# A two-layer graph transformer on one core: the gate's bias added by VectorE, its tangent taken in SBUF, and the attention terms turned ahead of the output projection

## The chip, the cores and the metric

The kernel runs on one core of a Trainium2 chip. The metric is the time of one execution on the device in microseconds. The profile names the engines PE (TensorE; PEld is its weight load), DVE (VectorE), ACT (ScalarE), POOL (GpSimd) and SP (SyncE, which only issues transfers here).

## What is computed

`x` is 64 graphs of 128 nodes with 384 features, `adj` a 128 x 128 mask for each. Two layers follow one another, each with a residual and a layer norm. The first is masked attention with 6 heads of 64. The second is a graph attention with 12 heads of 32 and a gate:

```
h = einsum('bnd,ade->bane', x1, W); th = tanh(h)
attn = th·w_src + swap(th·w_dst);  attn = where(attn >= 0, attn, 0.2 * attn); masked, softmax
feat = elu(attn @ h + b)
gate = sigmoid(x1 @ H_w.T + H_b)
y = layernorm(x1 + gate * feat + (1 - gate) * x1)
```

All is f32. Products that need the full precision are made as three products of a high and a low part (hi·hi, lo·hi, hi·lo).

## The kernel before

One graph is one tile of 128 nodes, and the 64 tiles are written out one after the other in the program of every engine: groups of four (`g`, `j` = 0 to 3), 18 rounds in all. In a round, TensorE makes the q, k and v projections of the next group (`qkv`; `fill_a`, `fill_b`), the first layer's attention of a tile (`att`, tile `ta`), the second layer's projections and logits of a tile two behind (`gat`, `tl` = `ta` - 2) and the end of the one behind that (`tail`). The rounds at the end have no `qkv`, then no `att`. The tile j = 3 makes four v projections where the others make one q or k projection each for `ps_a` and `ps_b`. Every engine works through its list in order, and semaphores that are waited for in that list bind the engines together. The order is written by hand.

The second layer of a tile, as far as the change touches it:

- TensorE turns the tile (`turn_x1`, L409), multiplies it into `ps_d` bank 1 (h, L253) and, in three chunks between other work, into `ps_d` bank 2 (the gate). Behind the last chunk a bfloat16 product adds the gate's bias, held as three bfloat16 rows (L429).
- ScalarE takes tanh of h (`th`, L633); GpSimd multiplies it with the two weight rows (`thw`, L999); VectorE sums it (L844) and splits the sums into three bfloat16 terms (L868 to L878, `sd3`).
- TensorE turns the terms (`turn_sd`, L435). ScalarE makes `rows_L` of them (L670, three), VectorE makes `cols_R` (L885, on partitions 64 to 127).
- TensorE makes the logits (L447): three products, one for each of the banks 0, 1 and 2 of `ps_d`. These banks hold the turned weights of the tile before (`turn_p1`, L459) until they have been copied to `p1T` (bank 0 by VectorE, L760; banks 1 and 2 by ScalarE, L593).
- ScalarE takes the tangent of half the gate from `ps_d` bank 2 (L661). VectorE uses `gate` two tiles later (L824).

The wait in the logits reads:

```
for q in range(3):
    pe.wait_ge(S["rows_ready"], 3 * t + q + 1)
    if due(t):
        pe.wait_ge(S[f"p1T_{q}"], t)
```

In the lists around it, `L362` turns the first layer's weights, after GpSimd has normalised them (L991); VectorE copies them (`p0T`, L830); `L742` makes the low parts of the turned tile and of the context; L747 and L752 evict q and k from `ps_b`; L891 to L895 begin the last norm of a tile, which GpSimd ends, and GpSimd's mask addition on the logits (L964) stands behind that. Twice a group GpSimd also waits for the terms (`sd3_ready`) before it adds a bias to the next input (L945), and once before it makes the low part of the next group's input (L916, two).

Of the kernel before, what the change touches and what calls it, by code (L numbers as in the profile page):

```python
# [29 lines left out]
ALU = mybir.AluOpType  # L30
# [18 lines left out]
def build_program(nc, xT_in, x, adj, Wq, bq, Wk, bk, Wv, bv, Wf, bf, W1, b1, w_src, w_dst, HwT, Hb,  # L49
                  ident_in, pick_in, out):  # L50
    with ExitStack() as ctx:
# [23 lines left out]
        ones_b = sb("ones_b", [P, P], BF16)  # L75
# [12 lines left out]
        hb_rows = sb("hb_rows", [P, D], BF16)  # L88
# [43 lines left out]
        def staging(buffer):  # L132
# [4 lines left out]
        hb_row = r1[0:1, :]  # L137
        hb_rest = y[0:1, :, :]
        hb_split = gate[0:1, :, :].rearrange("p a d -> p (a d)").bitcast(BF16)[:, 0:3 * D].rearrange("p (a d) -> p a d", a=3)
# [4 lines left out]
        names = """padding_ready ident_in_ready const_in weight_in_0 weight_in_1 weight_in_2 weight_in_3 weight_in_4 weight_in_5 late_hi bvf_made bf_ready adj_in x_in_ready weight_hi weight_lo mask_ready consts_ready pick_ready hb_moved  # L144
            bias_in bias_ready hb_small x_hi x_lo x_lo_first xb_in xb_ready q_made k_made qk_a_ready qk_b_ready v_made v_even v_odd
            scores_ready neg_ready exp0_ready inv0_ready p0_ready p0_turned p0T_even p0T_odd
            ctx_made ctx_hi ctx_lo out_made r0_ready mv0_ready ln0_small x1_ready
            x1_turned x1_hi x1_lo h_made h_ready th_ready gate_made gate_ready thw_ready
# [47 lines left out]
        def _(sp):  # L196
            sp.dma_start(x_cols[:], xT_in[0]).then_inc(S["x_in_ready"], 16)
            for n, name in enumerate(W_ORDER):
                if n == 4:
# [6 lines left out]
                    sp.dma_start(hb_row, Hb.rearrange("(o d) -> o d", o=1)).then_inc(S["const_in"], 16)  # L206
# [41 lines left out]
        def _(pe):  # L248
            def split_product(out_ap, lhs, rhs, chunks=range(C), closed=True):

                for c in chunks:
                    for k, (a, b) in enumerate(HI_LO):
                        last = pe.matmul(out_ap, lhs(a, c), rhs(b, c), start=(c == 0 and k == 0),  # L253
                                         stop=(closed and c == C - 1 and k == 2))
                return last
# [156 lines left out]
            def project_h(t, n, j):  # L412
# [3 lines left out]
                if isinstance(t, int) and t == 0:  # L416
                    pe.wait_ge(S["weight_lo"], 6)
                    pe.wait_ge(S["hb_moved"], 16)
# [4 lines left out]
            def project_gate(chunks):  # L423

                split_product(ps_d[:, 2, 0:D], lambda a, c: x1T[a][:, c, :],
                              lambda b, c: w_parts["hw"][b][:, c, :], chunks, closed=False)
# [23 lines left out]
            def turn_p1(t, next_is_here, groups):  # L450

                for q in groups:
                    if next_is_here and q == 1:
                        pe.wait_ge(S["h_ready"], t + 2)
                    if next_is_here and q == 2:
                        pe.wait_ge(S["gate_ready"], t + 2)
# [23 lines left out]
            def iteration(g, par, n):  # L480
                qkv, att = parts(n)
                for j in range(G):
# [50 lines left out]
        def _(act):  # L533
# [25 lines left out]
            def iteration(g, par, n):  # L559
# [36 lines left out]
                for j in range(G):  # L596
# [68 lines left out]
                    if gat:  # L665
# [25 lines left out]
        def _(dve):  # L691
# [19 lines left out]
            def small_constants():  # L711
# [4 lines left out]
                dve.wait_ge(S["padding_ready"], 2)  # L716
# [4 lines left out]

                dve.tensor_copy(hb_split[:, 0, :], hb_row).then_inc(S["hb_small"], 1)
                dve.wait_ge(S["hb_small"], 1)
                dve.tensor_tensor(hb_rest[:, 0, :], hb_row, hb_split[:, 0, :], ALU.subtract).then_inc(S["hb_small"], 1)
                dve.wait_ge(S["hb_small"], 2)
# [331 lines left out]
```

## Time and profile before

| | |
|---|---|
| median of 3 runs | 1132.04 us (1130.24 to 1132.44) |
| the profiled execution | 1132.1 us, span 1130.2 us |
| busy | PE 1073.2 us (95%), ACT 919.4 (81%), DVE 897.2 (79%), POOL 765.2 (68%) |
| mean granted clock of TensorE | 0.986 of full speed |

The time of an execution is a little longer than the span between its first and last instruction. Busy time is that in which an engine has an instruction under way. Matmuls are pipelined and the end of one is modelled, so TensorE can read as busy through a short wait; the starts of its products and weight loads tell more.

### The profile page before, as it was taken

What the parts mean: (1) busy time and instruction counts of PE and PEld (TensorE: products, weight loads), DVE (VectorE), ACT (ScalarE), POOL (GpSimd) and SP (SyncE); (2) the same over time, 40 slices, a digit from 0 to 9 for tenths busy, and PEclk for the clock granted to TensorE, in tenths of its full rate; (3) what the DMA queues carried; (4) which work ended last, traced back from release to release, by engine and by line L of the source; (5) the groups of instructions that cost most, each with busy time, mean ns of one, the idle gap of its engine ahead of it and who ended that gap; (6) DMA issues with size and microseconds to landing.
All of it is one profiled execution on the core that took longest, in us unless ns stands there. A gap on an engine that the chain in (4) does not pass through costs nothing.

```text
span 1130.2 us, 25501 instructions
## 1 busy us (share of the span) xinstructions
PE 1073.2 (95%) x8236; PEld 883.3 (78%) x8236; DVE 897.2 (79%) x1828; ACT 919.4 (81%) x3383; POOL 765.2 (68%) x909
## 2 busy tenths in 40 slices
PE   6889999999999999999999999999999999997774
PEld 5678888888888888878888888888888888786652
DVE  5457878888887888888788888878888887888874
ACT  3348888888888888888888888888888888888874
POOL 1367776676777667677766767776676777667652
PEclk9999999999999999999999999999999999999986
DMA  9101010020101002010100201010020101000000
GB/s 270 56 2 57 15 68 18 8 71 16 64 15 61 26 8 71 16 64 15 62 26 8 71 15 64 15 60 27 8 72 16 64 15 43 16 8 16 16 15 21
DMA packets 25893, 44.66 MB, mean 40 GB/s; under 512 B 2462, under 2 KB 23714, under 8 KB 25762
## 3 DMA queue, kind: packets, MB, share of 16 engines
q1 hardware_dynamic: 23234, 41.91, 10.9%
q10 hardware_dynamic: 2496, 1.12, 0.5%
q8 instruction: 68, 1.11, 0.4%
q14 instruction: 63, 0.52, 0.2%
q0 software_dynamic: 32, 0.00, 0.0%
HBM read 30.43 MB, written 12.58 MB: 38 GB/s over the span
## 4 chain that ended last, share of the span: by engine, by line
PE 57%; POOL 23%; issue 9%; DVE 6%; ACT 3%; DMA 2%; POOLq 0%; ACTq 0%; DVEq 0%
PE ps_b L253 13%; PE ps_d L253 13%; POOL z L964 9%; PE ps_a L253 7%; PE ps_d L459 5%; POOL xT_lo L916 4%; PE ps_a L382 3%; PE ps_s L362 3%; PE ps_s L354 3%; PE ps_d L447 3%; POOL p L991 3%; PE ps_c L469 2%; POOL s L956 2%; POOL thw L999 2%; POOL y L958 2%
## 5 line engine op out<-in xcount | busy, mean ns | idle before, releaser
L583 ACT ACTIVATE z<-z,s 128x128 f32<-128x128 f32 x768 | 297.1, 391 | 1.5 <-DVE s L798 0.9
L964 POOL TENSOR_TENSOR z<-z,mask 128x512 f32<-128x512 f32 x192 | 218.2, 1164 | 0.5 <-ACT z L679 0.5
L583 ACT ACTIVATION_READ_ACCUMULATOR z<-z,s 128x1 f32 x768 | 146.6, 191 | 0.0
L610 ACT ACTIVATE p<-ps_s,s 128x128 f32<-128x128 f32 x384 | 134.7, 378 | 13.1 <-DVE s L776 13.0
L991 POOL TENSOR_TENSOR p<-p,s 128x768 f32<-128x768 f32 x64 | 94.2, 1471 | 61.4 <-DVE s L804 61.4
L459 PE MATMUL ps_d<-ident,z 128*128 128x128 f32 x768 | 118.7, 278 | 9.2 <-ACT z L583 8.2
L953 POOL TENSOR_SCALAR s<-s 128x1 f32<-128x1 f32 x128 | 28.8, 225 | 143.3 <-DVE s L895 131.6
L999 POOL TENSOR_TENSOR thw<-th,w_sd 128x768 f32<-128x768 f32 x64 | 117.4, 1834 | 3.7 <-ACT th L633 3.7
L459 PEld LDWEIGHTS ps_d<-ident,z 128*128 128x128 f32 x768 | 90.6, 143 | 17.6 <-ACT z L583 9.1
L679 ACT ACTIVATE z<-ps_d 128x512 f32<-128x512 f32 x192 | 100.8, 598 | 1.2 <-PE ps_d L447 1.2
L945 POOL TENSOR_TENSOR xb<-xb,bf_all 128x768 f32<-128x768 f32 x32 | 58.6, 1834 | 58.6 <-DVE sd L878 55.5
L601 ACT ACTIVATE x1T_hi<-ps_b 128x384 fp32r<-128x384 f32 x64 | 31.4, 491 | 76.0 <-PE ps_b L409 76.0
L798 DVE TENSOR_REDUCE s<-z 128x8 f32<-128x1024 f32 x64 | 77.7, 1213 | 18.0 <-POOL z L964 18.0
L830 DVE COPY p0T<-ps_s 128x384 f32<-128x384 f32 x64 | 35.7, 557 | 62.4 <-PE ps_s L362 62.4
L916 POOL TENSOR_TENSOR xT_lo<-x_cols,xT_hi 128x768 fp32r<-128x768 f32 x30 | 58.4, 1969 | 39.4 <-DVE sd L878 32.6
L610 ACT ACTIVATION_READ_ACCUMULATOR p<-ps_s,s 128x1 f32 x384 | 84.1, 219 | 0.0
L253 PE MATMUL ps_d<-hw_hi,x1T_hi 128*128 128x384 f32 x192 | 82.8, 431 | 0.0
L253 PE MATMUL ps_b<-wf_hi,ctxT_hi 128*128 128x384 f32 x192 | 78.9, 411 | 2.8 <-DVE ctxT_lo L742 1.3
L956 POOL TENSOR_TENSOR s<-s,minus_half 128x1 f32<-128x1 f32 x128 | 72.5, 566 | 10.6
L593 ACT ACTIVATE p1T<-ps_d 128x512 f32<-128x512 f32 x128 | 75.0, 586 | 0.7 <-PE ps_d L459 0.7
L776 DVE TENSOR_REDUCE s<-ps_s 128x6 f32<-128x768 f32 x64 | 61.2, 956 | 16.2 <-PE ps_s L354 12.8
L253 PE MATMUL ps_d<-w_hi,x1T_hi 128*128 128x384 f32 x192 | 66.2, 345 | 7.0 <-DVE x1T_lo L742 7.0
(154 smaller groups left out, 3448.5 us busy)
## 6 DMA issues: line engine op xcount, KB each, us to landing
x_cols<-in_xT_dram SPq DMA_DIRECT2D x16, 768.0 KB, 6.4
xb<-in_x_dram SPq DMA_DIRECT2D x16, 768.0 KB, 4.9
out_dram<-y SPq DMA_DIRECT2D x64, 192.0 KB, 1.8
z<-in_L_gnn_Wq_dram SPq DMA_DIRECT2D x1, 576.0 KB, 6.4
p1T<-in_L_gnn_Wk_dram SPq DMA_DIRECT2D x1, 576.0 KB, 8.7
qT<-in_L_gnn_Wv_dram SPq DMA_DIRECT2D x1, 576.0 KB, 11.1
kT<-in_L_gnn_Wf_dram SPq DMA_DIRECT2D x1, 576.0 KB, 13.4
z<-in_L_gnn_W_dram SPq DMA_DIRECT2D x1, 576.0 KB, 11.7
```

The source lines that it names most:

```text
L253: last = pe.matmul(out_ap, lhs(a, c), rhs(b, c), start=(c == 0 and k == 0), stop=(closed and c == C - 1 and k == 2))
L459: last = pe.transpose(ps_d[:, q, (a % 4) * N:(a % 4 + 1) * N], z[:, a, :], ident[:])
L583: done = act.activation(z[:, a, :], z[:, a, :], ACT.Exp, bias=neg1[:, a:a + 1], accum_out=sum1[:, a:a + 1])
L593: act.activation(p1T[:, 4 * q:4 * q + 4, :], ps_d[:, q, :].rearrange("p (a n) -> p a n", a=4), ACT.Copy).then_inc(S[f"p1T_{q}"], 1)
L610: last = act.activation(p0[:, o, i, :], ps_s[:, o, i * N:(i + 1) * N], ACT.Exp, bias=neg0[:, k:k + 1], accum_out=sum0[:, k:k + 1])
L679: act.activation(z[:, 4 * q:4 * q + 4, :], ps_d[:, q, :].rearrange("p (a n) -> p a n", a=4), ACT.Prelu, alpha=0.2).then_inc(S["z_ready"], 1)
L798: dve.tensor_reduce(neg1[:, 0:8], z[:, 0:8, :], AX_X, ALU.max, negate=True).then_inc(S["neg1_ready"], 1)
L916: pool.tensor_tensor(xT[1][:, :, at], x_cols[:, :, at], xT[0][:, :, at].bitcast(F32), ALU.subtract).then_inc(S["x_lo"], 1)
L956: pool.tensor_tensor(rs, ve, minus_half[:], ALU.pow).then_inc(S[small], 1)
L964: pool.tensor_tensor(z[:, 4 * q:4 * q + 4, :], z[:, 4 * q:4 * q + 4, :], mask[:, t, :].unsqueeze(1).broadcast_to([P, 4, N]), ALU.add).then ...
L991: pool.tensor_tensor(p0[:].rearrange("p o i n -> p (o i) n"), p0[:].rearrange("p o i n -> p (o i) n"), inv0.unsqueeze(2).broadcast_to([P, ...
L999: pool.tensor_tensor(thw[:], th[:].unsqueeze(1).broadcast_to([P, 2, D]), w_sd[:], ALU.mult).then_inc(S["thw_ready"], 1)
```

## The change

The gate's bias is no longer a product. It is loaded to all 128 partitions (`hb_all`), VectorE adds it as it evicts bank 2 of `ps_d`, and ScalarE takes the tangent in place in SBUF at the end of its tile. The three bfloat16 rows of the bias, their preparation on VectorE and the transfer on GpSimd's queue are gone. VectorE copies bank 1 of the turned weights, after `cols_R`. VectorE evicts q, k or v ahead of the copy of `p0T`, and splits the terms ahead of the context's low part. TensorE turns the terms ahead of the output projection.

```diff
@@ sync
-                    sp.dma_start(hb_row, Hb.rearrange("(o d) -> o d", o=1)).then_inc(S["const_in"], 16)
+                    sp.dma_start(hb_all[:], Hb.partition_broadcast(P)).then_inc(S["const_in"], 16)
@@ tensor
-                pe.matmul(ps_d[:, 2, 0:D], ones_b[:], hb_rows[:], start=False, stop=True
-                          ).then_inc(S["gate_made"], 1)
+                last.then_inc(S["gate_made"], 1)
@@ logits, and turn_p1 for q == 2
-                pe.wait_ge(S["gate_ready"], t + 1)
+                pe.wait_ge(S["gate_summed"], t + 1)
@@ tensor, iteration
                         project_gate((2,))
+                    if gat:
+                        turn_sd(tl)
                     if att:
                         project_out(ta, g, j, n, (0, 1))
-                    if gat:
-                        turn_sd(tl)
@@ scalar, iteration
-                        act.wait_ge(S["gate_made"], tl + 1)
-                        if due(tl - 2):
-                            act.wait_ge(S["tail_small"], 3 * (tl - 2))
-                        act.activation(gate[:, tl % 3, :], ps_d[:, 2, 0:D], ACT.Tanh,
-                                       scale=0.5).then_inc(S["gate_ready"], 1)
-                    if tail:
-                        turned_p1(tl - 1, 1)
...
+                    if gat:
+                        act.wait_ge(S["gate_summed"], tl + 1)
+                        act.activation(gate[:, tl % 3, :], gate[:, tl % 3, :], ACT.Tanh,
+                                       scale=0.5).then_inc(S["gate_ready"], 1)
@@ vector, small_constants
-                dve.tensor_copy(hb_split[:, 0, :], hb_row).then_inc(S["hb_small"], 1)
...
-                dve.tensor_copy(hb_split[:, 2, :], hb_rest[:, 1, :]).then_inc(S["hb_small"], 1)
@@ vector, iteration (ahead of the copy of p0T)
+                        dve.wait_ge(S["gate_ready"], t2 + 1)
                         dve.scalar_tensor_tensor(r1[:], gate[:, t2 % 3, :], 1.0, ps_r, ALU.add, ALU.mult
                                                  ).then_inc(S["tail_small"], 1)
+                    if qkv and j == 0:
+                        evacuate_q(1)
...
+                    elif qkv:
+                        evacuate_v(3)
@@ vector, iteration (behind the terms)
+                    if att:
+                        dve.wait_ge(S["ctx_made"], ta + 1)
+                        lo_part(ctxT, ps_a, slice(0, N), "ctx_hi", ta + 1, "ctx_lo")
+                    if gat:
+                        dve.wait_ge(S["gate_made"], tl + 1)
+                        if due(tl - 2):
+                            dve.wait_ge(S["tail_small"], 3 * (tl - 2))
+                        dve.tensor_tensor(gate[:, tl % 3, :], ps_d[:, 2, 0:D], hb_all[:], ALU.add
+                                          ).then_inc(S["gate_summed"], 1)
                     if tail:
                         turned_p1(tt, 0)
...
+                    if tail:
+                        turned_p1(tt, 1)
@@ gpsimd, moved_constants
-                pool.dma_start(hb_rows[0:3, :], hb_split[:]).then_inc(S["hb_moved"], 16)
```

On VectorE, in the middle of an ordinary tile with a k projection (kT is its eviction), behind L824 of before, there stood:

```order
L830 COPY p0T<-ps_s 128x384
L838 TENSOR_TENSOR h<-ps_d,b_all 128x384
L844 TENSOR_REDUCE sd<-thw 128x24
L752 TENSOR_SCALAR kT<-ps_b,bk_col 128x512
L742 TENSOR_TENSOR ctxT_lo<-ps_a,ctxT_hi 128x384
L868 CAST sd<-sd 128x2x12
L870 TENSOR_TENSOR sd_rest<-sd 128x24
L873 CAST sd<-sd_rest 128x2x12
L875 TENSOR_TENSOR sd_rest<-sd_rest,sd 128x24
L878 CAST sd<-sd_rest 128x2x12
```

At the same place, behind the same instruction (now L801), there stands now:

```order
L729 TENSOR_SCALAR kT<-ps_b,bk_col 128x512
L815 COPY p0T<-ps_s 128x384
L823 TENSOR_TENSOR h<-ps_d,b_all 128x384
L829 TENSOR_REDUCE sd<-thw 128x24
L842 CAST sd<-sd 128x2x12
L844 TENSOR_TENSOR sd_rest<-sd 128x24
L847 CAST sd<-sd_rest 128x2x12
L849 TENSOR_TENSOR sd_rest<-sd_rest,sd 128x24
L852 CAST sd<-sd_rest 128x2x12
L719 TENSOR_TENSOR ctxT_lo<-ps_a,ctxT_hi 128x384
```

The eviction has moved to the front of the stretch and the context's low part to its end; the ten instructions are the same.

On VectorE directly behind that stretch, up to the last norm, there stood:

```order
L760 COPY p1T<-ps_d 128x512
L885 TENSOR_TENSOR cols_R<-ps_c,choose 64x512
L891 SCALAR_TENSOR_TENSOR r<-r,x 128x384
L893 BN_STATS s<-r 128x6
L895 BN_AGGR s<-s 128x2
```

and there stands now:

```order
L860 TENSOR_TENSOR gate<-ps_d,hb_all 128x384
L737 COPY p1T<-ps_d 128x512
L868 TENSOR_TENSOR cols_R<-ps_c,choose 64x512
L737 COPY p1T<-ps_d 128x512
L876 SCALAR_TENSOR_TENSOR r<-r,x 128x384
L878 BN_STATS s<-r 128x6
L880 BN_AGGR s<-s 128x2
```

The gate's addition has come in front of the copy of bank 0, and the copy of bank 1 between `cols_R` and the last norm.

On TensorE, from the last product of the gate to the logits of a tile (ps_b is the output projection, ident,z the turns of bank 2), there stood:

```order
L253 MATMUL ps_d<-hw_lo,x1T_hi 128x384
L429 MATMUL ps_d<-hb_rows,ones_b 128x384
L253 MATMUL ps_b<-wf_hi,ctxT_hi 128x384
L253 MATMUL ps_b<-wf_hi,ctxT_lo 128x384
L253 MATMUL ps_b<-wf_lo,ctxT_hi 128x384
L253 MATMUL ps_b<-wf_hi,ctxT_hi 128x384
L253 MATMUL ps_b<-wf_hi,ctxT_lo 128x384
L253 MATMUL ps_b<-wf_lo,ctxT_hi 128x384
L435 MATMUL ps_c<-ident_b,sd 128x128
L459 MATMUL ps_d<-ident,z 128x128 x4
```

and there stands now:

```order
L249 MATMUL ps_d<-hw_lo,x1T_hi 128x384
L428 MATMUL ps_c<-ident_b,sd 128x128
L249 MATMUL ps_b<-wf_hi,ctxT_hi 128x384
L249 MATMUL ps_b<-wf_hi,ctxT_lo 128x384
L249 MATMUL ps_b<-wf_lo,ctxT_hi 128x384
L249 MATMUL ps_b<-wf_hi,ctxT_hi 128x384
L249 MATMUL ps_b<-wf_hi,ctxT_lo 128x384
L249 MATMUL ps_b<-wf_lo,ctxT_hi 128x384
L452 MATMUL ps_d<-ident,z 128x128 x4
```

The bias product is gone, and the turn of the terms stands in its place instead of six products later.

## Rows read from the trace of the kernel before

**Rows 1.** Windows: stretch, length, busy us (instructions) PE, PEld, DVE, ACT, POOL; PEclk, DMA.

```profile
521.15:536.99 15.84, 15.84 (x124) 12.93 (x125) 13.70 (x29) 13.77 (x53) 11.83 (x15) 1.00 0.03 12
536.99:554.95 17.96, 17.96 (x143) 15.76 (x143) 14.03 (x30) 15.46 (x56) 11.71 (x15) 1.00 0.04 14
554.95:571.28 16.33, 16.14 (x126) 12.93 (x125) 13.86 (x29) 13.97 (x53) 12.46 (x15) 1.00 0.32 109
```

**Rows 2.** Timeline of TensorE in one tile: start, length, engine, line, what, [idle before].

```profile
530.23 0.39 PE L253 MATMUL ps_b<-xT_lo,wk_hi 128*128 128x512 f32 x1
530.46 0.82 PE L362 MATMUL ps_s<-ident,p 128*128 128x128 f32 x6
...
534.40 0.34 PE L253 MATMUL ps_d<-hw_lo,x1T_hi 128*128 128x384 f32 x1
534.58 0.34 PE L429 MATMUL ps_d<-hb_rows,ones_b 128*128 128x384 bf16 x1
...
536.99 0.96 PE L447 MATMUL ps_d<-cols_R,rows_L 128*128 128x512 bf16 x3
537.79 0.49 PE L344 MATMUL ps_s<-mask,ident_b 128*128 128x384 bf16 x2
```

**Rows 3.** Timelines of ScalarE and of the weight loads, end of that tile.

```profile
536.85 0.58 ACT L593 ACTIVATE p1T<-ps_d 128x512 f32<-128x512 f32 x1
...
537.54 0.10 PEld L447 LDWEIGHTS ps_d<-cols_R,rows_L 128*128 128x128 bf16 x1 [0.36 <-issue]
```

**Rows 4.** Timeline of VectorE, that tile, with L891 of the one before.

```profile
520.93 0.86 DVE L891 SCALAR_TENSOR_TENSOR r<-r,x 128x384 f32<-128x384 f32 x1
...
529.91 0.55 DVE L824 SCALAR_TENSOR_TENSOR r<-gate,ps_c 128x384 f32<-128x384 f32 x1
531.32 0.56 DVE L830 COPY p0T<-ps_s 128x384 f32<-128x384 f32 x1 [0.85 <-PE ps_s L362]
531.79 0.55 DVE L838 TENSOR_TENSOR h<-ps_d,b_all 128x384 f32<-128x384 f32 x1
532.25 0.94 DVE L844 TENSOR_REDUCE sd<-thw 128x24 f32<-128x768 f32 x1
533.11 0.74 DVE L752 TENSOR_SCALAR kT<-ps_b,bk_col 128x512 f32<-128x512 f32 x1
533.82 0.56 DVE L742 TENSOR_TENSOR ctxT_lo<-ps_a,ctxT_hi 128x384 fp32r<-128x384 f32 x1
534.29 0.17 DVE L868 CAST sd<-sd 128x24 bf16<-128x24 f32 x1
...
535.23 0.68 DVE L760 COPY p1T<-ps_d 128x512 f32<-128x512 f32 x1
536.08 0.69 DVE L885 TENSOR_TENSOR cols_R<-ps_c,choose 64x512 bf16<-64x512 bf16 x1 [0.18 <-PE ps_c L435]
536.81 0.84 DVE L891 SCALAR_TENSOR_TENSOR r<-r,x 128x384 f32<-128x384 f32 x1
```

**Rows 5.** Timeline of VectorE in a late tile, where L885 had nothing to wait for.

```profile
1089.27 0.68 DVE L760 COPY p1T<-ps_d 128x512 f32<-128x512 f32 x1
1089.98 0.69 DVE L885 TENSOR_TENSOR cols_R<-ps_c,choose 64x512 bf16<-64x512 bf16 x1
```

**Rows 6.** Timelines of GpSimd, VectorE and TensorE, tiles j = 3 and j = 0.

```profile
553.47 3.94 POOL L916 TENSOR_TENSOR xT_lo<-x_cols,xT_hi 128x768 fp32r<-128x768 f32 x2 [2.40 <-DVE sd L878]
...
556.35 0.18 DVE L895 BATCH_NORM_AGGREGATE s<-s 128x2 f32<-128x6 f32 x1
...
564.65 0.88 PE L362 MATMUL ps_s<-ident,p 128*128 128x128 f32 x6 [0.17 <-POOL p L991]
```

**Rows 7.** Timeline of TensorE at the start.

```profile
34.70 0.81 PE L328 MATMUL ps_s<-wf_lo,bv_col 128*128 128x384 f32 x2
37.54 0.52 PE L344 MATMUL ps_s<-mask,ident_b 128*128 128x384 bf16 x2 [2.04 <-DVE bf_all L859]
```

**Rows 8.** Timeline of TensorE in a tile without projections.

```profile
1040.76 0.87 PE L362 MATMUL ps_s<-ident,p 128*128 128x128 f32 x6 [1.66 <-POOL p L991]
```

More of the change, by code:

```diff
@@ L87, in build_program @@
         w_sd = sb("w_sd", [P, 2, D])
-        hb_rows = sb("hb_rows", [P, D], BF16)
+        hb_all = sb("hb_all", [P, D])
         mask = sb("mask", [P, B, N], BF16)
@@ L136, in build_program @@
         bf_in = th[:]
-        hb_row = r1[0:1, :]
-        hb_rest = y[0:1, :, :]
-        hb_split = gate[0:1, :, :].rearrange("p a d -> p (a d)").bitcast(BF16)[:, 0:3 * D].rearrange("p (a d) -> p a d", a=3)
         adj_u8 = x1[:].rearrange("p a j d -> p (a j d)")[:, 0:B * N // 4].bitcast(mybir.dt.uint8
                                                                           ).rearrange("p (b n) -> p b n", n=N)
-        names = """padding_ready ident_in_ready const_in weight_in_0 weight_in_1 weight_in_2 weight_in_3 weight_in_4 weight_in_5 late_hi bvf_made bf_ready adj_in x_in_ready weight_hi weight_lo mask_ready consts_ready pick_ready hb_moved
-            bias_in bias_ready hb_small x_hi x_lo x_lo_first xb_in xb_ready q_made k_made qk_a_ready qk_b_ready v_made v_even v_odd
+        names = """padding_ready ident_in_ready const_in weight_in_0 weight_in_1 weight_in_2 weight_in_3 weight_in_4 weight_in_5 late_hi bvf_made bf_ready adj_in x_in_ready weight_hi weight_lo mask_ready consts_ready pick_ready
+            bias_in bias_ready x_hi x_lo x_lo_first xb_in xb_ready q_made k_made qk_a_ready qk_b_ready v_made v_even v_odd
             scores_ready neg_ready exp0_ready inv0_ready p0_ready p0_turned p0T_even p0T_odd
             ctx_made ctx_hi ctx_lo out_made r0_ready mv0_ready ln0_small x1_ready
-            x1_turned x1_hi x1_lo h_made h_ready th_ready gate_made gate_ready thw_ready
+            x1_turned x1_hi x1_lo h_made h_ready th_ready gate_made gate_summed gate_ready thw_ready
             sd_ready split_small sd3_ready sd_turned rows_ready cols_ready logits_ready z_ready zm_ready neg1_ready
@@ L248, in _, with split_product @@
         def _(pe):
-            def split_product(out_ap, lhs, rhs, chunks=range(C), closed=True):
+            def split_product(out_ap, lhs, rhs, chunks=range(C)):
                 for c in chunks:
@@ L253, in split_product @@
                         last = pe.matmul(out_ap, lhs(a, c), rhs(b, c), start=(c == 0 and k == 0),
-                                         stop=(closed and c == C - 1 and k == 2))
+                                         stop=(c == C - 1 and k == 2))
                 return last
@@ L423, in project_gate @@
             def project_gate(chunks):
-                split_product(ps_d[:, 2, 0:D], lambda a, c: x1T[a][:, c, :],
-                              lambda b, c: w_parts["hw"][b][:, c, :], chunks, closed=False)
+                last = split_product(ps_d[:, 2, 0:D], lambda a, c: x1T[a][:, c, :],
+                                     lambda b, c: w_parts["hw"][b][:, c, :], chunks)
                 if chunks[-1] == C - 1:
-                    pe.matmul(ps_d[:, 2, 0:D], ones_b[:], hb_rows[:], start=False, stop=True
-                              ).then_inc(S["gate_made"], 1)
+                    last.then_inc(S["gate_made"], 1)
             def turn_sd(t):
@@ L455, in turn_p1 @@
                     if next_is_here and q == 2:
-                        pe.wait_ge(S["gate_ready"], t + 2)
+                        pe.wait_ge(S["gate_summed"], t + 2)
                     pe.wait_ge(S["exp1_ready"], 3 * t + q + 1)
@@ L715, in small_constants @@
                 dve.wait_ge(S["const_in"], 16 * 7)
-                dve.wait_ge(S["padding_ready"], 2)
+                dve.wait_ge(S["padding_ready"], 1)
                 dve.tensor_copy(rows_L[64:P, :, :], of_bank[64:P, :].unsqueeze(2).broadcast_to([64, 3, N])
@@ L822, in iteration @@
                             dve.wait_ge(S["y_ready"], t2)
+                        dve.wait_ge(S["gate_ready"], t2 + 1)
                         dve.scalar_tensor_tensor(r1[:], gate[:, t2 % 3, :], 1.0, ps_r, ALU.add, ALU.mult
                                                  ).then_inc(S["tail_small"], 1)
+                    if qkv and j == 0:
+                        evacuate_q(1)
+                    elif qkv and j == 1:
+                        evacuate_k(0)
+                    elif qkv and j == 2:
+                        evacuate_k(2)
+                    elif qkv:
+                        evacuate_v(3)
                     if att:
@@ L845, in iteration @@
                                           ALU.add).then_inc(S["sd_ready"], 1)
-                    if qkv and j == 0:
-                        evacuate_q(1)
-                    elif qkv and j == 1:
-                        evacuate_k(0)
-                    elif qkv and j == 2:
-                        evacuate_k(2)
-                    elif qkv:
-                        evacuate_v(3)
                     if n == 0 and j < 3:
@@ L932, in moved_constants @@
             def moved_constants():
-                pool.wait_ge(S["hb_small"], 5)
-                pool.wait_ge(S["padding_ready"], 2)
-                pool.dma_start(hb_rows[0:3, :], hb_split[:]).then_inc(S["hb_moved"], 16)
                 pool.wait_ge(S["const_in"], 16 * 7)
```

16 lines of the change are left out of this document (removed).

## Prediction

> **What bounds the kernel now.** I read windows one tile long, then each engine's timeline inside one tile. In the windows, each from one tile's logits to the next, TensorE is busy for the whole of an ordinary tile and of the long tile (j = 3), at the full granted clock, while VectorE and ScalarE have about 2 us over [rows 1]. So a tile costs what stands in TensorE's queue, plus the waits inside that queue which the busy share hides. One such wait is at the logits: their three products (L447) begin 6.53 us after the turns of L362, and the mask product of L344 follows 0.80 us behind [rows 2]. The third weight load of L447 comes at 537.54, 0.36 us idle, 0.11 us after ScalarE's copy of bank 2 has ended (536.85 + 0.58 = 537.43) [rows 3]. The logits overwrite the banks that these copies empty, so that copy holds the third product.
>
> The exception is the tile j = 0: 16.33 us, about 0.45 above an ordinary one. There L362 waits for GpSimd's L991, whose queue had the two long L916 of the tile before in it [rows 1, 6].
>
> **The change, on a clock that starts with L362 (530.46 is 0).** All is taken from the one profiled execution, 1132.1 us with a span of 1130.2; the median shown is 1132.04, so the two are one number here.
>
> *TensorE.* L429 goes. The last gate product is 0.18 us ahead of it, and so much it occupies itself, since every product of this width does; the turn of the terms only changes places with the output products. TensorE's own work falls by 0.18 a tile [rows 2]: 64 x 0.18 = 11.5 us if nothing else moves.
>
> *ScalarE* loses the tangent from its place and the copy of bank 1 (0.58, as its copy of bank 2), and so starts the rows and the copy of bank 2 sooner [rows 3]. The turns of bank 2 stay about where they are and its copy ends near 6.3 instead of 6.97: the old hold is gone. The tangent comes back at the end of the tile. No row has it in SBUF at this width; it costs more than nothing and no more than the 0.58 of a wider copy (I take the upper end), and it lies in ScalarE's spare 2 us [rows 1], so nothing of it is on the path. Were that cover gone, it would cost 0.6 a tile.
>
> *VectorE* gets the copy of bank 1 and the gate's addition. Where do they end? The eviction of q or k waits for the last product ahead of L362, which starts 0.23 before zero and lasts 0.39 [rows 2], so it starts near 0.2; L824 has ended at 0.00 and does not hold it. The steps from start to start [rows 4]: eviction 0.71, p0T 0.47, h 0.46, sums 0.86, the five terms 0.94. That puts p0T at 0.9 to 1.5 and the end of the terms at 3.75. TensorE reads p0T some 1.7 after zero and wants the terms at 4.12, where L429 stood: both are in time. The low part of the context runs 3.65 to 4.2; TensorE asks for it just then, and a delay of up to 0.15 is swallowed by the next wait.
>
> The gate's addition cannot start before the last gate product is out: it starts at 3.94 and lasts 0.34 [rows 2], with 0.04 for the release 4.32. It is an addition from PSUM, 384 wide, like h: 0.46 to the next start. Then come, in this order, the copy of bank 0, cols_R and the copy of bank 1. A copy ahead of cols_R takes 0.71 start to start [rows 5], cols_R 0.73 (536.08 to 536.81), and the copy lasts 0.68 [rows 4]. End: 4.32 + 0.46 + 0.71 + 0.73 + 0.68 = 6.90. With the 0.11 of [rows 3] the **second** product of the logits loads at 7.01. Before, the **third** loaded at 7.08 and L344 came 0.25 later. Now one more product lies between, 0.21 (three with the hold in them took 0.80, and a product as wide takes 0.23 at L253 [rows 2]): 7.01 + 0.21 + 0.25 = 7.47 against 7.33. **The hold is not removed, it moves one product forward, and an ordinary tile becomes 0.14 longer**; the 0.18 of L429 is lost in the wait.
>
> Two steps of that chain hang on one property. Pairs of VectorE instructions with nothing to wait for overlap by some 0.08 (0.46 for the 0.55 of h), the pairs around cols_R do not (0.71 for 0.68, 0.73 for 0.69) [rows 4, 5]. The Trainium skill, "VectorE: DVE Perf Modes", section "Two Vector instructions with no wait between them", gives a model for it: an instruction that starts in another quadrant of partitions than the one before it is held until that one has finished, and cols_R works on partitions 64 to 127. By that rule, the trace agrees. Without a hold the two steps would be about 0.60 and 0.61, the copy would end at 6.67 and the sum be the first rival's.
>
> Is VectorE's loop too long? The steps give L891 a start of 6.83 where it had 6.35. From L891 to the end of L824 it took 9.53 (520.93 to 530.46), of which 0.3 is L891's own surplus over other instructions of this width [rows 4]. VectorE is then free 16.05 to 16.35 after zero, and is needed 0.2 behind the next zero, at 16.2. It holds, with a tenth to spare or none.
>
> *GpSimd.* The terms are done about 1.1 us sooner (4.85 to 3.75), and L916 waits for them. Behind it stands the second norm, which needs the statistics of L895: L916 ended at 557.41, L895 at 556.53 [rows 6]. L895 comes 0.5 later, at about 557.05, so GpSimd gains some 0.35, and L991 lets L362 start near 564.3 instead of 564.65, about when TensorE is ready. The 0.45 of the j = 0 tile is recovered.
>
> **Sum.** A group of four tiles: 4 x 0.14 - 0.45 = +0.11 us; 15 groups, nearly +2. In the last group, without projections, L362 waits 1.66 us for L991 [rows 8], and that loop runs through L891: four tiles by 0.43 (0.48 less the little room ahead of L798) = +1.7. The last gated tile, with no other work around it, carries the addition and two copies before L891: 0.46 + 0.71 + 0.61 - 0.34 (L429) = +1.4, and ScalarE's shorter queue gives some 0.3 back. At the start five small instructions go from in front of L859. TensorE's wait of 2.04 for it shrinks until the products of L328 are out at 35.5: -1.3; the wider load of the bias, 128 rows of 1.5 KB in place of one, ahead of two weights of 576 KB, takes some back, and the first gated tile, where the terms come late, gives some; I let these two cancel [rows 7]. Total +2 + 1.7 + 1.4 - 0.3 - 1.3 = +3.5: **1135.5**.
>
> **Rivals.**
> 1. *The chain behind the gate is quicker, down to no hold around cols_R.* 0.23 sooner turns +0.14 into -0.09: 15 x (-0.36 - 0.45) = -12, the end +2, the start -1.3: 1121. Every 0.1 us of this chain is 6 us of the kernel; from about 0.06 on it decides for a gain. At its far end the copy is out by 6.45, the three products run through in 0.65 from 6.35, L344 comes at 7.00, and the kernel at 1105. For it: durations vary by hundredths. Against: rows 5.
> 2. *VectorE is full.* If L891 stays at its surplus and one more instruction grows as much beside GpSimd's long additions, its loop passes the tile by 0.3 to 0.4 and three of four tiles follow: 15 x (1.2 + 0.14 - 0.45) = +13, 1147 with the end. For it: there is no room. Against: what is added reads PSUM, and L945, which ran beside L891, moves away with the terms.
> 3. *Nothing measurable.* With the chain 0.04 to 0.06 quicker the sums cancel: 1132.
>
> **How the numbers follow.** My case, 1133 to 1142, has 0.45; rival 1 with what lies between has 0.28; rival 2 has 0.09; rival 3 has 0.18. A change under 0.2% (2.3 us) can't be told from none here. So faster 0.28, within 0.2% 0.2, slower 0.52. The range runs from 1119, just past rival 1's first number, to 1143, short of rival 2; less than 2 in 10 is outside.
>
> **What would show it.** Right: the second weight load of the logits idle until 0.1 us behind VectorE's copy of bank 1; terms done by 3.8 on the clock; the gate's addition waiting for TensorE; no wait of L362 at j = 0; ordinary tiles of 16.0. Wrong: logits that run through (tiles of 15.5), or VectorE without a single wait in a tile. The forecast fails first if the addition, cols_R or the copies take other times than their rows.

## The result: 2.4% slower, and the profile after

The changed kernel takes 1161.73 us (median of 4, 1156.82 to 1162.12) against 1132.24: a ratio of 1.0245, 95% interval 1.0221 to 1.027. The forecast was 1135.5 with 1119 to 1143. The profiled execution is the fastest of the four, 1156.82 with a span of 1155.0. So the trace explains 24.8 us (1155.0 against 1130.2); the other executions show some 5 more, at a lower mean granted clock (0.972 to 0.974 instead of 0.976).

Windows of the changed kernel, again from one tile's logits to the next; the first and the last two answer to [rows 1]:

```profile
512.34:528.43 16.09, 15.81 (x124) 13.03 (x124) 14.74 (x31) 13.45 (x52) 11.86 (x14) 1.00 0.04 14
...
544.54:562.69 18.15, 18.11 (x143) 15.93 (x142) 15.02 (x32) 15.40 (x55) 12.82 (x15) 1.00 0.03 12
562.69:579.19 16.50, 15.86 (x124) 12.92 (x123) 15.11 (x31) 13.43 (x52) 10.87 (x14) 1.00 0.32 110
```

Three things are to be seen. Each kind of tile is about 0.2 us longer. In the ordinary tile TensorE is no longer busy throughout (15.81 of 16.09). VectorE's busy time, 13.70 to 14.03 before, is 14.74 to 15.11.

One ordinary tile of the changed kernel follows. Its clock starts with L358 (521.74), which was L362. VectorE's and GpSimd's timelines:

```profile
521.94 0.75 DVE L729 TENSOR_SCALAR kT<-ps_b,bk_col 128x512 f32<-128x512 f32 x1
...
524.51 0.18 DVE L842 CAST sd<-sd 128x24 bf16<-128x24 f32 x1
524.72 0.37 DVE L844 TENSOR_TENSOR sd_rest<-sd 128x24 f32<-128x24 f32 x1
...
525.64 0.55 DVE L719 TENSOR_TENSOR ctxT_lo<-ps_a,ctxT_hi 128x384 fp32r<-128x384 f32 x1
526.11 0.55 DVE L860 TENSOR_TENSOR gate<-ps_d,hb_all 128x384 f32<-128x384 f32 x1
526.57 0.68 DVE L737 COPY p1T<-ps_d 128x512 f32<-128x512 f32 x1
527.29 0.69 DVE L868 TENSOR_TENSOR cols_R<-ps_c,choose 64x512 bf16<-64x512 bf16 x1
528.01 0.69 DVE L737 COPY p1T<-ps_d 128x512 f32<-128x512 f32 x1
```

```profile
524.37 0.69 POOL L938 TENSOR_SCALAR x<-r,s 128x384 f32<-128x384 f32 x1
```

TensorE, its weight loads and ScalarE in the same tile:

```profile
526.34 0.41 PE L249 MATMUL ps_b<-wf_hi,ctxT_hi 128*128 128x384 f32 x1 [0.25 <-DVE ctxT_lo L719]
...
528.43 1.01 PE L440 MATMUL ps_d<-cols_R,rows_L 128*128 128x512 bf16 x3
529.28 0.49 PE L340 MATMUL ps_s<-mask,ident_b 128*128 128x384 bf16 x2
```

```profile
528.82 0.22 PEld L440 LDWEIGHTS ps_d<-cols_R,rows_L 128*128 128x128 bf16 x2 [0.30 <-issue]
```

```profile
528.10 0.60 ACT L586 ACTIVATE p1T<-ps_d 128x512 f32<-128x512 f32 x1 [0.80 <-PE ps_d L452]
```

The bank-1 copy ends at 528.70 (6.96 after zero, forecast 6.90), the second weight load follows 0.12 later, and L340 stands at 7.54 (forecast 7.47, before 7.33). The hold has moved one product forward, as the forecast said. New is the wait of 0.25 ahead of the output projection: VectorE's low part of the context is late, because one subtraction of the split (L844) took 0.37 instead of 0.18. It ended at 525.09; GpSimd's L938, which had started before it, ended at 525.06. Two of the signs that I had named did not come: the terms are done at 3.99 and not by 3.8, and the gate's addition does not wait for TensorE but follows the low part without a pause (526.11, 4.37 after zero).

### The profile page after: what moved, and what is told of

The parts are those of the page before. It is cut to its first block, busy times and chain, and to the rows that moved or that the text cites. A ratio compares the mean times of both kernels' runs of the same rounds, so it can differ in the third digit from the quotient of the medians.

```text
span 1155.0 us, 25428 instructions
## 1 busy us (share of the span) xinstructions
PE 1076.2 (93%) x8172; PEld 893.3 (77%) x8172; DVE 973.7 (84%) x1951; ACT 899.4 (78%) x3319; POOL 762.5 (66%) x906
## 3 DMA queue, kind: packets, MB, share of 16 engines
q1 hardware_dynamic: 23376, 42.10, 10.6%
## 4 chain that ended last, share of the span: by engine, by line
PE 59%; DVE 23%; issue 8%; POOL 8%; ACT 2%; DMA 0%; DVEq 0%; POOLq 0%; ACTq 0%
PE ps_b L249 18%; PE ps_a L249 10%; PE ps_d L249 9%; POOL z L944 4%; DVE sd L829 4%; PE ps_d L452 3%; PE ps_s L350 3%; PE ps_d L440 3%; PE ps_c L462 3%; DVE p1T L737 2%; DVE ctxT_lo L719 2%; PE ps_c L470 2%; PE ps_s L358 2%; DVE sd_rest L844 2%; DVE p0T L815 2%
## 5 line engine op out<-in xcount | busy, mean ns | idle before, releaser
L452 PEld LDWEIGHTS ps_d<-ident,z 128*128 128x128 f32 x768 | 97.0, 144 | 21.2 <-ACT z L576 11.1
L737 DVE COPY p1T<-ps_d 128x512 f32<-128x512 f32 x128 | 87.9, 687 | 3.4 <-PE ps_d L452 1.5
L249 PE MATMUL ps_b<-wf_hi,ctxT_hi 128*128 128x384 f32 x192 | 75.5, 393 | 15.8 <-DVE ctxT_lo L719 14.0
L586 ACT ACTIVATE p1T<-ps_d 128x512 f32<-128x512 f32 x64 | 38.3, 599 | 52.3 <-PE ps_d L452 52.3
L249 PE MATMUL ps_d<-w_hi,x1T_hi 128*128 128x384 f32 x192 | 65.9, 343 | 7.0 <-DVE x1T_lo L719 7.0
L901 POOL TENSOR_TENSOR xT_lo<-x_cols,xT_hi 128x768 fp32r<-128x768 f32 x30 | 54.4, 1830 | 23.9 <-DVE sd L852 16.7
L440 PE MATMUL ps_d<-cols_R,rows_L 128*128 128x512 bf16 x192 | 63.3, 384 | 6.3 <-DVE p1T L737 4.1
```

Of the source, the lines that this page charges most:

```text
L440: last = pe.matmul(heads, rows_L[:, q, :], cols_R[:], start=True, stop=True)
L452: last = pe.transpose(ps_d[:, q, (a % 4) * N:(a % 4 + 1) * N], z[:, a, :], ident[:])
L737: dve.tensor_copy(p1T[:, 4 * q:4 * q + 4, :], ps_d[:, q, :].rearrange("p (a n) -> p a n", a=4)).then_inc(S[f"p1T_{q}"], 1)
```

## Experiments

The change has three parts: **A**, the order (terms split ahead of the context's low part and turned ahead of the output projection, evictions ahead of p0T); **B**, VectorE copies bank 1; **C**, the gate (no L429, VectorE's addition, the tangent in SBUF). With before and after, six kernels give all eight combinations. The table has, for each, the time and the usual interval from one start of cols_R to the next in VectorE's timeline: the two ordinary ones, j = 3, j = 0, their sum, the second gated tile at the start, and a tile without projections (end).

| kernel | us | ordinary | j=3 | j=0 | four | second | end |
|---|---|---|---|---|---|---|---|
| before | 1132.2 | 15.87, 15.88 | 17.96 | 16.28 | 66.0 | 17.13 | 15.0 |
| A | 1129.2 | 15.76, 15.79 | 17.86 | 15.96 | 65.4 | 20.04 | 15.24 |
| B | 1165.2 | 16.14, 16.15 | 18.25 | 17.18 | 67.7 | 17.13 | 17.26 |
| C | 1142.7 | 16.04, 16.04 | 18.26 | 16.22 | 66.6 | 17.61 | 15.30 |
| A+C | 1132.2 | 15.86, 15.72 | 17.82 | 16.45 | 65.9 | 19.86 | 15.22 |
| A+B | 1139.1 | 15.80, 15.81 | 17.77 | 16.65 | 66.0 | 20.05 | 15.35 |
| B+C | 1182.3 | 16.48, 16.49 | 18.69 | 17.07 | 68.7 | 17.60 | 17.48 |
| A+B+C, after | 1161.7 | 16.09, 16.09 | 18.15 | 16.50 | 66.8 | 19.74 | 17.13 |

In the last column all four tiles at the end agree within 0.1, except in three kernels. In B and in the changed kernel three of them read so and one 15.8; in B+C two read 17.5 and two 16.0 to 16.1. Experiment 8 is about this difference.

**1. After without B.**

```diff
 (VectorE, behind cols_R)
-                    if tail:
-                        turned_p1(tt, 1)
 (ScalarE, ahead of the rows)
+                    if tail:
+                        turned_p1(tl - 1, 1)
```

> The changed kernel with one thing undone: the copy of the turned bank 1 goes back to ScalarE, at its old place. Theory H (the hold in my prediction: the second logits product waits for VectorE's bank-1 copy, 6.96 after the tile's zero): that product loads earlier, the third is held by ScalarE's bank-2 copy, the ordinary tile falls from 16.09 to about 15.90, and the time from 1161.5 to about 1151. Theory C (the context's low part, put behind the terms, holds the output projection by 0.25 and with it the turns of bank 2): ScalarE's bank-2 copy still ends at about 6.96, the tile stays at 16.0 to 16.1, and the time at 1158 to 1162.

1132.24, ratio to before 1.0 (0.9984 to 1.0016). TensorE, same place in the tile (zero at 531.88):

```profile
538.39 0.82 PE L440 MATMUL ps_d<-cols_R,rows_L 128*128 128x512 bf16 x3
539.05 0.49 PE L340 MATMUL ps_s<-mask,ident_b 128*128 128x384 bf16 x2
```

The three products run through, L340 comes at 7.17 after zero instead of 7.54, and 29.5 us are gone: theory H by sign, and three times its size. The wait for the low part, in 40 tiles of the changed kernel between 100 and 1000 us (11.5 us), is left in 14 (4.6 us), though its place in the order is the same. So the low part's new place alone does not make the loss, and theory C falls.

**2. After without A.** The three moves of the diff reversed on VectorE, and on TensorE:

```diff
-                    if gat:
-                        turn_sd(tl)
                     if att:
                         project_out(ta, g, j, n, (0, 1))
+                    if gat:
+                        turn_sd(tl)
```

> The changed kernel with the order undone: VectorE's evictions of q, k and v behind the sums again, the context's low part ahead of the terms, the terms turned behind the output projection. Theory C: the wait of the output projection (14.0 us in all) goes, the ordinary tile falls to about 15.9, the time to 1148 to 1152. Theory H: VectorE's bank-1 copy has as much ahead of it as in the changed kernel, so it still ends near 6.96, and the time stays at 1158 to 1163; the tile j=0 and the end stay as they are or get longer by up to 0.5 each.

1182.3, 1.044 (1.0424 to 1.0456): neither theory, but 21 slower. The new order is no cause of the loss, it is what limits it.

**3 and 4. After without C, and C alone.** Their edits are the diff's parts on the gate, taken out of after or put into before.

> The changed kernel with the gate's half undone: the ones-row product is back on TensorE (0.18 of a tile), ScalarE's tangent reads the bank, VectorE adds no bias (0.46 less ahead of its copies). Theory V (VectorE's chain from the eviction to the bank-1 copy sets the tile, whatever is in it): the chain gets 0.46 shorter, of which 0.18 to TensorE: tile 15.85 to 15.95, loop at j=0 and at the end shorter by 0.3 to 0.5, time 1138 to 1147. Theory C: the gate's addition stands behind the context's low part and so has no part in the wait: 1158 to 1163.

1139.09, 1.0053 (1.0036 to 1.007): the time of theory V. Not each part of it came: ordinary tiles read 15.80, just under its range, and the tile j = 0 got 0.15 longer (16.65) where it was to get shorter.

> The kernel before with the gate's half of the change alone: no ones-row product, VectorE evicts the gate with its bias added, the tangent follows in SBUF; order and copies as before. Theory V: 0.46 more on VectorE ahead of the bank-0 copy and cols_R, whose late end now holds the first product: ordinary tile +0.1 to +0.2, the loop at the end +0.4 per tile, time 1140 to 1150. Rival (VectorE has that time to spare while bank 1 is ScalarE's): TensorE's 0.18 and ScalarE's 0.2 come out, 1124 to 1133.

1142.69, 1.0095 (1.0072 to 1.0119). Theory V again. The product that leaves TensorE brings the output projection only 0.04 forward (4.12 after L362 instead of 4.16), and behind it the logits start 0.37 later (2.74 after it instead of 2.37), because cols_R now stands behind VectorE's addition.

**5 and 6. B alone and A alone.**

> The kernel before with one part of the change: VectorE copies the turned bank 1, behind cols_R. Measured so far: this part costs 29 us when the other two are there (1161.5 against 1132.2). Theory V (a budget: VectorE has some room from the context's low part to its last write that TensorE waits for, and each added instruction beyond that room lengthens every tile): without the order's 0.3 to 0.7 earlier start and without the gate's 0.46, the copy's 0.70 lands between gate_back (1139) and twice that excess: 1145 to 1160. Rival (the parts only hurt together): 1130 to 1137.

1165.15, 1.0291 (1.0274 to 1.0308), above the range of theory V. Timeline of TensorE, and its chief wait in the whole kernel (total, times, longest):

```profile
535.52 0.59 PE L447 MATMUL ps_d<-cols_R,rows_L 128*128 128x512 bf16 x2 [0.62 <-DVE p1T L758]
```

```profile
PE ps_d L447 <- DVE p1T L758: 39.2, 63, 0.9
```

> The kernel before with the order alone: terms split ahead of the context's low part and turned ahead of the output projection, evictions ahead of p0T. Theory V: bank_1_on_ScalarE with the gate's part as well was 1132.2, with 2.7 of it lost at the second gated tile, where the first cast of the terms takes 1.92 beside GpSimd's mask of 1.90; the steady tile gains up to 0.15, so 1127 to 1132 with a loss of 2 to 3 at that tile again (19.6 to 20.1 instead of 17.1). Rival (the late low part holds the output projection and the tile with it): steady tile +0.1 to +0.25, 1138 to 1146.

1129.21, 0.9966 (0.9955 to 0.9978): 3 us faster, in spite of 2.9 us lost at the second gated tile. In the steady tiles A is worth 0.6 of a group.

**7. After without B, masks behind.** GpSimd's order is as it was, only its wait for the terms now stands ahead of the mask too:

```diff
-                    if 0 <= ta - 1 < 3:
-                        mask_quarter(ta)
                     if gat and qkv and j > 0:
                         pool.wait_ge(S["sd3_ready"], tl + 1)
+                    if 0 <= ta - 1 < 3:
+                        mask_quarter(ta)
```

> The kernel with the copy of bank 1 back on ScalarE, and GpSimd's three later quarters of the mask put behind its wait for the finished terms, so that none of them runs beside the split. Theory P (the cast and the subtraction on VectorE can't end before GpSimd's instruction that overlaps them ends: 73.08 for a mask that ends at 73.06): the first casts in the second and third gated tile take 0.18 instead of 1.92 and 1.80, TensorE has no gap there and its granted clock stays 1.00, the tile is 17.1 to 17.6 instead of 19.86, the time 2 to 4 less than 1132.2. Rival (these casts take so long from another cause): no change, 1131 to 1134.

1129.83, 0.9981 (0.9966 to 0.9996), and the second interval is 16.98. This is what went away, in the changed kernel at the first gated tile (after without B has the cast there instead, 1.92 beside a mask of 1.90). VectorE and GpSimd:

```profile
70.77 1.75 DVE L844 TENSOR_TENSOR sd_rest<-sd 128x24 f32<-128x24 f32 x1
```

```profile
70.58 1.91 POOL L912 TENSOR_SCALAR mask<-x 128x2048 bf16<-128x2048 uint8 x1
```

In this experiment:

```profile
70.91 0.18 DVE L844 CAST sd<-sd 128x24 bf16<-128x24 f32 x1
...
71.35 0.18 DVE L849 CAST sd<-sd_rest 128x24 bf16<-128x24 f32 x1
```

A subtraction of 24 columns takes 0.18, or it ends 0.03 after GpSimd's instruction ends (72.52 and 72.49). In all fourteen traces, every small cast or subtraction that took over 0.25 ended 0.01 to 0.04 behind a GpSimd instruction. In the changed kernel TensorE ran dry behind this (1.76 idle ahead of the turn of the terms, at 73.22), and its granted clock over 70 to 80 us was 0.83; here it is 1.00 in each window from 70 to 85 us. Theory P.

The Trainium skill, "SBUF — State Buffer", section "Who interferes with whom", tells of a port pair that VectorE and GpSimd hold in turn, each for a whole instruction, where VectorE's has two inputs in SBUF or is a fast copy. By that rule, the trace agrees for the subtraction, which has two inputs in SBUF, and for VectorE's instructions that read PSUM, which do not wait (p0T's copy takes 0.55 or 0.56 in all 64 tiles of the changed kernel). It agrees for the casts only in part: in the ordinary tile above, L842 started 0.14 behind L938 and still took 0.18. Which casts wait stays open.

**8. After, its end filled.**

```diff
                         project_h(tl, n, j)
+                    if gat and att and not qkv:
+                        split_product(ps_d[:, 2, 0:D], lambda a, c: x1T[a][:, c, :],
+                                      lambda b, c: w_parts["hw"][b][:, c, :])
```

> The changed kernel with the gate's nine products done twice in the two gated tiles j that have attention but no projections (n = 16), first in the gap of 2.07 in which TensorE waits for GpSimd's p; the repeated ones are overwritten. Nothing is left out. Theory K (the 1.3 that three of these tiles take more than 15.83 is the granted clock of 0.90 in them): at least two of the tiles fall from 17.1 to about 15.9, the time by 2 to 5. Rival (the 17.1 come from waits, and the slower products are hidden): the tiles stay, the time stays within 1160 to 1163.

1154.76 (1153.88 to 1159.41), 1.0207 (1.0182 to 1.0233): by the medians 7 less than the changed kernel, with nine products more in each of the four tiles of that round. The executions of the two kernels overlap, though, and the profiled one here is the longest (1159.41, its first cols_R 4.5 later by the start, which the edit does not touch). What the traces place in the four tiles is 3.9 us. These tiles read 15.87, 15.81, 15.83, 15.81 where the changed kernel has 17.16, 15.83, 17.12, 17.15. A window of the filled kernel:

```profile
1062.00:1079.00 17.00, 14.74 (x122) 12.36 (x124) 15.13 (x32) 13.07 (x52) 11.14 (x14) 1.00 0.04 13
```

Windows of the changed kernel (the first is its full-clock tile), and its context products in the tile of the second and third window:

```profile
1046.45:1062.28 15.83, 11.98 (x105) 9.25 (x103) 14.29 (x29) 12.92 (x50) 9.96 (x13) 1.00 0.04 14
...
1062.00:1079.00 17.00, 13.72 (x108) 10.94 (x107) 14.35 (x30) 12.92 (x51) 9.96 (x13) 0.90 0.03 13
...
1073.40:1076.40 3.00, 3.00 (x19) 2.25 (x19) 2.83 (x8) 1.94 (x10) 2.34 (x5) 0.50 0.02 5
```

```profile
1074.71 1.55 PE L378 MATMUL ps_a<-p0T,v 128*64 128x128 f32 x12
```

Filled, these take 0.88, as in the kernel before. So the 1.3 us of each long tile is a stretch of 3 us with TensorE at its lower level (0.50, 1.2 GHz), which begins 1.1 us after an idle time of 2.07 ahead of L358; theory K. Filled, that idle time is 0.50. B alone and B+C, whose tiles there are 17.3 and 17.5, show 0.90 too. The idle time is not the whole condition: the tile of 15.83 has the same 2.07 ahead of L358 and kept 1.00.

**9. A+C, the gate added twice** (a second copy into a buffer that nobody reads).

```diff
+                        dve.tensor_tensor(junk[:], ps_d[:, 2, 0:D], hb_all[:], ALU.add)
                         dve.tensor_tensor(gate[:, tl % 3, :], ps_d[:, 2, 0:D], hb_all[:], ALU.add
                                           ).then_inc(S["gate_summed"], 1)
```

> The kernel with the copy of bank 1 back on ScalarE (1132.2), in which VectorE does the gate's addition twice: once more, 0.46, into a buffer that nobody reads, ahead of the bank-0 copy and cols_R. Theory V (what counts is the sum of VectorE's work from the eviction to its last write that TensorE waits for, 6.20 after the zero there, and it has no more than about 0.3 of room): cols_R ends at 6.66 and holds the first product, ordinary tile from 15.72 to 15.95 or 16.2, j=0 and each tile of the end +0.46, time 1143 to 1155. Rival (the loss needs the bank-1 copy itself, of 0.70, in this place): tiles +0.1 at most, 1132 to 1137.

1151.97, 1.0171 (1.0156 to 1.0187). 0.46 us of useless work reproduces the lengths of the changed kernel's steady tiles to 0.03: 16.06, 16.07, 18.16, 16.50, without a bank-1 copy on VectorE (the end's tiles do not follow: 15.57). VectorE and TensorE in an ordinary tile with zero 523.44:

```profile
523.64 0.75 DVE L732 TENSOR_SCALAR kT<-ps_b,bk_col 128x512 f32<-128x512 f32 x1 [0.32 <-PE ps_b L250]
...
529.40 0.69 DVE L872 TENSOR_TENSOR cols_R<-ps_c,choose 64x512 bf16<-64x512 bf16 x1
```

```profile
527.96 0.41 PE L250 MATMUL ps_b<-wf_hi,ctxT_hi 128*128 128x384 f32 x1 [0.17 <-DVE ctxT_lo L722]
...
530.31 0.81 PE L441 MATMUL ps_d<-cols_R,rows_L 128*128 128x512 bf16 x3
```

The three products run through here; they are held as a whole. Cols_R, behind the added work, ends at 530.09, and they start 2.35 after the output projection where A+C has 2.09: +0.26. The projection itself starts 0.10 later after zero, because the first cast of the split took 0.28 beside GpSimd's norm. Together this is the 0.35 by which the tile grew over A+C. VectorE's loop as a whole is not full in this tile: its eviction (L732) waits 0.32 for TensorE. What has hardly any room is the stretch from the eviction to the last of VectorE's writes that the logits need: with the bank-1 copy in it the second product is held, with the added work the first.

**10. After, the norm behind the terms** in j = 1 and j = 2.

```diff
-                    if 0 <= ta - 1 < B:
+                    late = gat and (qkv and j in (1, 2))
+                    if 0 <= ta - 1 < B and not late:
                         first_norm(ta - 1)
 ...
                         pool.wait_ge(S["sd3_ready"], tl + 1)
+                    if 0 <= ta - 1 < B and late:
+                        first_norm(ta - 1)
```

> The changed kernel with GpSimd's first normalisation put behind its wait for the terms in the tiles j=1 and j=2, so that it can't run beside the split there (in the changed kernel the first subtraction takes 0.37, and ends 0.03 after GpSimd's 0.69 for the norm; it takes 0.18 where the norm ends before it). Theory P: it takes 0.18, VectorE's later work starts 0.19 earlier, the output projection's wait of 0.25 mostly goes, and these two tiles fall by 0.15 to 0.25 to 15.85 to 15.95, the time from 1161.7 to 1154 to 1157. Rival (TensorE's tile is set by the bank-1 copy alone and the stretched subtraction is no part of it): tiles stay 16.09, 1160 to 1163.

1157.92, 1.0222 (1.0208 to 1.0236): by the medians 3.8 less, between the two ranges. The traces do not show this gain: the profiled execution took 1157.22, against 1156.82 for the changed kernel. The subtraction took 0.18 in these tiles, but they read 16.04 and 16.31, against 16.09 twice. TensorE and VectorE in a tile with zero 519.75:

```profile
526.82 0.59 PE L440 MATMUL ps_d<-cols_R,rows_L 128*128 128x512 bf16 x2 [0.17 <-DVE p1T L737]
```

```profile
526.70 1.10 DVE L876 SCALAR_TENSOR_TENSOR r<-r,x 128x384 f32<-128x384 f32 x1
```

The bank-1 copy still holds the second product, L340 comes at 7.50, and the collision comes back further down: L876, with both inputs in SBUF, takes 1.10 instead of 0.56 beside GpSimd's shifted queue. In j = 1 the low part comes in time. In j = 2 it is late again, because L876's surplus has come round through the loop: the eviction starts 0.53 after L358 instead of 0.20. In the steady tiles theory P as to time is wrong here, and its rival is nearer, though the time lies below the rival's range too. What the trace gains, 1.3 at the second gated interval (18.46 instead of 19.74) and 1.5 ahead of the first cols_R, it loses again in the steady tiles (0.2 a group) and at the end, where now all four tiles read 17.2 at a granted clock of 0.90.

**11 and 12. A alone with the mask behind; the same with the norm behind** in j = 1, 2 and the tiles without projections.

> The kernel before with the order alone (1129.2) and GpSimd's three later mask quarters behind its wait for the terms. Theory P (the cast waits out GpSimd's instruction beside it): the second gated tile falls from 20.04 to about 17.1, the time to 1125.5 to 1127. Rival (it comes back as a later wait): 1128.5 to 1130.

1124.33, 0.9925 (0.9912 to 0.9937): theory P, 1.2 us below its range; the second gated interval is 16.83.

> The kernel with the order alone and the masks behind, with GpSimd's first normalisation behind its wait for the terms in the tiles j=1 and j=2 and in those without projections. Theory P: in the end's tiles a cast of 0.52 becomes 0.18, these four fall from 15.24 to about 14.9, another 1.3 off the time of the kernel without this step (so 1124 to 1126); the steady tiles, where casts take 0.18 already, stay at 15.78. Rival (the later norm comes back as a wait for x1 or for r0's buffer): the steady tiles get longer by 0.1 or more, time above 1129.

1121.66, 0.9902 (0.9888 to 0.9915): faster than both kernels, by 10.6 and 40 us, and 2.3 below the range of theory P. The end's tiles fall from 15.24 to 14.93, the steady ones stay at 15.73 and 15.79. VectorE and GpSimd in an end's tile of A alone:

```profile
1042.77 0.54 DVE L870 CAST sd<-sd_rest 128x24 bf16<-128x24 f32 x1
```

```profile
1042.60 0.68 POOL L958 TENSOR_SCALAR x<-r,s 128x384 f32<-128x384 f32 x1
```

and VectorE's in the last kernel:

```profile
1037.16 0.18 DVE L870 CAST sd<-sd_rest 128x24 bf16<-128x24 f32 x1
```

## Why the prediction was wrong, step by step

**Right: the hold moves one product forward.** Copy, load and L340 came within 0.07 us of the forecast; an ordinary tile got 0.22 longer instead of 0.14, and the long one 0.19. The 0.07 more is the stretched subtraction with the low part behind it, or the hold without it: experiment 10 took the one away and the other stayed. L429's 0.18 was lost in the wait as forecast, and the tangent in SBUF (0.52) cost nothing that shows.

**The step that failed: "The 0.45 of the j = 0 tile is recovered", with "It holds, with a tenth to spare or none" behind it.** The forecast had +0.11 for a group, the trace +0.84 (66.83 against 65.99). Of these 0.73, the tile j = 0 has 0.53 (+0.22 where -0.31 was forecast) and the three others 0.20. Over the 14 groups between the second cols_R and the end's tiles this is +11.7 us. GpSimd's additions did end sooner, and TensorE's wait for L991 did go. But the next stretch is late. Timelines of VectorE, GpSimd and TensorE in that tile of the changed kernel:

```profile
562.98 0.94 DVE L876 SCALAR_TENSOR_TENSOR r<-r,x 128x384 f32<-128x384 f32 x1
...
572.05 0.55 DVE L801 SCALAR_TENSOR_TENSOR r<-gate,ps_c 128x384 f32<-128x384 f32 x1
...
575.30 0.53 DVE L844 TENSOR_TENSOR sd_rest<-sd 128x24 f32<-128x24 f32 x1
```

```profile
564.82 0.23 POOL L933 TENSOR_SCALAR s<-s 128x1 f32<-128x1 f32 x1 [1.31 <-DVE s L880]
...
575.10 0.70 POOL L938 TENSOR_SCALAR x<-r,s 128x384 f32<-128x384 f32 x1
```

```profile
572.07 0.82 PE L358 MATMUL ps_s<-ident,p 128*128 128x128 f32 x6
...
577.08 0.41 PE L249 MATMUL ps_b<-wf_hi,ctxT_hi 128*128 128x384 f32 x1 [0.32 <-DVE ctxT_lo L719]
```

Two delays add up. The first is VectorE's loop. GpSimd now waits for the statistics behind the two copies and the addition (1.31), and L876 had taken 0.94 instead of 0.56 beside GpSimd's L901 (as L891 did at this place before); the maxima, and r1's steps up to L801, come after it; so the eviction starts 0.45 after L358 instead of 0.20. The second is the split: its first subtraction took 0.53 instead of 0.18, to 0.03 behind the end of GpSimd's norm. The output projection starts 5.01 after L358, where it is 4.42 in tiles without either: 0.25 and 0.35 make up the difference. In an ordinary tile L876 starts at 7.00 (forecast 6.83) and L801 ends 0.13 after the next zero, and the eviction still starts at 0.20. There the loop did hold, and the low part is late by the stretched subtraction alone (0.19).

A alone shows neither delay at j = 0 (the eviction starts at 0.20, each instruction of the split takes 0.18 to 0.22) and does recover 0.32 of the 0.45; B or C takes it back (0.69 or 0.49 on top of A), with a subtraction of 0.45 to 0.53 in A+B and in A+C. The arithmetic on GpSimd's queue was right for the order, and I had added the other parts' work on VectorE as if nothing behind it would move.

So the mechanism was near that of my second rival (chance 0.09, 1147), but not by its account. It asked for one more instruction that grows beside GpSimd's long additions, and then for three of four tiles to follow. The instruction that grew is in the split and stands beside GpSimd's norm, and the loop passes the tile only at j = 0. I had argued "what is added reads PSUM", which is true of the added instructions. The split does not read PSUM. Before, it started 3.83 after L362 in an ordinary tile, when the norm had ended (2.84). A moved it to 2.77, and the later statistics move the norm: it ends at 2.85 in A alone and at 3.33 in the changed kernel.

**The size that failed: "four tiles by 0.43", "the last gated tile +1.4".** The end cost +11.9 us (six intervals of 100.0 against 89.1, and 25.7 against 24.7 behind the last cols_R), where the forecast had +2.8. The loop through L876 got 0.83 longer per tile at the full clock (15.83 against 15.0), not 0.43: the sum left out the split, where a small instruction costs 0.3 beside the norm (15.24 to 14.93 in experiment 12). And three of these tiles lost another 1.3 to the clock, which the forecast did not weigh at all. The four tiles have 7.2 of the 11.9. Of the rest, 3.7 lie in the last two intervals; the last one took 17.79 at a granted clock of 0.54, against 15.49 at 0.80, and no run separates the added work from the clock there.

**The start.** The first cols_R comes 1.4 sooner (74.12 against 75.53; -1.3 forecast), but the second gated interval is 2.6 longer, by the mask. That the first of these fits the forecast is partly luck: in experiment 8, whose program is the same up to there, it comes at 78.61. I had let the start's other effects cancel. Tiles +11.7, end +11.9, start +1.2 make up the 24.8 of the profiled execution.

**Not settled.** Parts do not add: C costs 10 alone and 3 on top of A, 17 on top of B and 23 on top of A+B. The tiles of a kernel settle into a pattern in which one delay covers another (experiment 8 reads 16.25 and 16.09 for the two ordinary tiles, which its edit does not touch, where the changed kernel has 16.09 twice), so a single price per instruction does not exist here. No run takes the stretched subtraction out of the tile j = 0 alone, so how much each of its two delays is worth by itself is read from one trace. What the four executions of the changed kernel lose beyond the profiled one I have put to the clock by its mean alone.

## What to carry to other kernels

When work goes to an engine that is busy for 14 of 16 us, do not go by its busy share. Take each of its writes that another engine waits for, follow the release through each queue that it passes into the next tile, and ask what a surplus of 0.1 us would do, and which instructions it would push beside each other. Try the parts of such a change apart: here one third of it was a gain that the other two buried. In this kernel the small VectorE instructions within SBUF belonged where GpSimd was idle. A wait on GpSimd could put them there at no cost in experiments 7, 11 and 12; in experiment 10 it only moved the collision.

## What the runs showed of the hardware

A VectorE instruction of 0.18 us took 0.37, 0.54, 1.75 and up to 1.95 (A alone) beside a GpSimd instruction, each time to 0.01 to 0.04 behind its end; a cast that started 0.14 behind such an instruction took 0.18 all the same. And TensorE's granted clock fell to 0.50 for 3 us behind an idle time of 2.07 to 2.14 in three of the four tiles at the changed kernel's end; the fourth, with 2.07, kept 1.00. Nine products put into that idle time kept the clock at 1.00 in all four, and these tiles became 3.9 us shorter with the extra work in them.
